# Every sixth partition: where the six blocks of two stacked operands lie in on-chip memory

## The reference, cut to what matters

```python
scores = jnp.einsum('bihd,bjhd->bhij', q, k) * d ** (-0.5)
scores = jnp.where(mask, scores, NEG)
p = jax.nn.softmax(scores, axis=-1)
o = jnp.einsum('bhij,bjhd->bihd', p, v)
```

## Time and profile before

| what | value |
|---|---|
| median of 3 runs | 423.71 us (423.14 to 424.17) |
| the profiled execution | 425.81 us |
| its span, from the first to the last instruction | 424.0 us |
| mean granted TensorE clock | 0.891 of full speed |
| busy in the span: TensorE, DVE, ACT, POOL | 314.1, 276.9, 164.7, 122.7 us |
| the queue of SP's DMAs | 42.12 MB in 50,211 packets |

### The profile page before, as it was taken

The page is one execution under the profiler, slowest core; times in us unless marked ns, Lnnn a source line. Parts: engine busy times, 40 slices in busy tenths (PEclk is TensorE's granted clock), DMA queues, the critical chain, the costliest instruction groups (busy, mean ns, idle before and its releaser), DMA issues. The chain is left out here.

```text
span 424.0 us, 5771 instructions
## 1 busy us (share of the span) xinstructions
PE 314.1 (74%) x1762; PEld 205.0 (48%) x1762; DVE 276.9 (65%) x865; ACT 164.7 (39%) x332; POOL 122.7 (29%) x105
## 2 busy tenths in 40 slices
PE   0797647628376479998899999997352988997982
PEld 0586546517143255555455555554341775444641
DVE  3868899565549188877614345354948959558694
ACT  1423512330012032322365665654302667757610
POOL 2654535547102011111104253343345000000023
PEclk9999879877568599999999999999795889898798
DMA  8992299968889837465543435006008000000011
GB/s 274 305 283 51 94 120 198 130 177 202 127 183 118 178 105 169 134 183 152 152 139 90 140 82 142 22 2 199 0 2 254 9 2 0 0 0 0 2 49 49
DMA packets 52545, 47.88 MB, mean 113 GB/s; under 512 B 5282, under 2 KB 50204, under 8 KB 52509
## 3 DMA queue, kind: packets, MB, share of 16 engines
q1 hardware_dynamic: 50211, 42.12, 43.4%
q0 software_dynamic: 1872, 4.22, 3.3%
q10 hardware_dynamic: 432, 1.18, 1.0%
HBM read 35.44 MB, written 15.87 MB: 121 GB/s over the span
## 5 line engine op out<-in xcount | busy, mean ns | idle before, releaser
L501 POOL DMA_INDIRECT yt_dram<-ysb,x x23 | 23.0, 1001 | 125.9 <-ACT ysb L617 87.2
L673 ACT ACTIVATE PT<-bank 128x512 f32<-128x512 f32 (+1 forms) x88 | 44.8, 558 | 21.5 <-PE bank L1177 20.8
L889 DVE TENSOR_REDUCE mx<-bank 128x1 f32<-128x384 f32 (+3 forms) x88 | 52.2, 637 | 1.2 <-PE bank L1159 0.5
L1158 PE MATMUL bank<-KS,QS 112*128 112x128 bf16 (+3 forms) x128 | 35.0, 322 | 12.9 <-DVE mx L889 11.6
L1032 DVE SCALAR_TENSOR_TENSOR s<-th,bank 128x176 f32<-128x176 f32 x23 | 7.7, 336 | 43.8 <-ACT th L705 43.7
L1788 PE MATMUL lbank<-u,w_ai 128*128 128x512 f32 x72 | 33.0, 619 | 1.9 <-issue 1.9
L1176 PE MATMUL bank<-QS,KS 115*128 115x512 bf16 (+3 forms) x128 | 31.1, 302 | 2.7 <-ACT PT L673 1.1
L1491 POOL TENSOR_TENSOR left<-xn,x 128x256 f32<-128x256 f32 x8 | 7.0, 898 | 86.7 <-DVE xn L1718 86.7
L507 POOL TENSOR_TENSOR small<-small,mhalf 128x16 f32<-128x16 f32 x8 | 24.4, 3046 | 17.3 <-DVE small L935 17.3
L1158 PEld LDWEIGHTS bank<-KS,QS 112*128 112x128 bf16 x128 | 12.7, 100 | 30.8 <-DVE mx L889 26.3
L1159 PE MATMUL bank<-tri,ident_b 128*128 128x128 bf16 x128 | 25.5, 227 | 0.0
(11 more groups left out here) (280 smaller groups left out, 808.7 us busy)
## 6 DMA issues: line engine op xcount, KB each, us to landing
wr<-w_dram SPq DMA_DIRECT2D x12, 352.0 KB
wt<-w_dram SPq DMA_DIRECT2D x11, 352.0 KB
QS<-parts_dram SPq DMA_DIRECT2D x12, 256.0 KB
KS<-parts_dram SPq DMA_DIRECT2D x12, 256.0 KB, 9.0
xs_dram<-x SPq DMA_DIRECT2D x1, 2967.0 KB, 15.3
x<-xs_dram SPq DMA_DIRECT2D x23, 129.0 KB, 2.2
w_dram<-in_w_chunks_dram SPq DMA_DIRECT2D x11, 256.0 KB, 4.8
wr<-in_w_chunks_dram SPq DMA_DIRECT2D x12, 176.0 KB
```

Source lines behind the costliest of these rows:

```text
L501: pool.indirect_dma_start(yt_dram, bass.IndirectOffsetOnAxis(ap=xg[:, n % XBUF, D:D + 1].bitcast(I32), axis=0), ysb[:, n % 2, :], None, bo ...
L673: act.activation(PT[:, k % 8, 0:n], bank[k % 2][:, 0:n], ACT.Exp, scale=float(DH) ** -0.5).then_inc(P_ready, 1)
L889: dve.tensor_reduce(mx[:, b * TB + i, heads[0]:heads[-1] + 1], bank[k % 2][:, 0:len(heads) * n].rearrange("p (h n) -> p h n", n=n), AX.X, ...
L1158: pe.matmul(out, QS[0:R_MAX, b, h, i * P:(i + 1) * P], KS[0:R_MAX, b, h, 0:n], start=True, stop=False)
```

## The change

The six blocks of 16 rows no longer take 16 neighbouring partitions each. Row d of block k goes to partition k + 6d in both stacks, so that the blocks interleave over partitions 0 to 95. Everything else, the rows from 96 on too, stays.

```diff
                     src = [parts_dram[b, which, level].rearrange("h d t -> d h t") for level in range(3)]
                     for block, (of_q, of_k) in enumerate(BLOCKS):
-                        rows = slice(block * DH, (block + 1) * DH)
+                        rows = slice(block, R_BIAS, len(BLOCKS))
                         if which == 0:
                             sp.dma_start(QS[rows, b, :, :], src[of_q]).then_inc(q_stacked[b], 16)
                         else:
                             sp.dma_start(KS[rows, b, :, :], src[of_k]).then_inc(k_stacked[b], 16)
```

## The result

The changed kernel takes 408.12 us (median of four executions, 407.47 to 409.56) against 423.42 for the kernel before on the same chip (421.56 to 424.17): a ratio of 0.965, 95% interval 0.961 to 0.969, so 15.3 us. The profiled execution takes 409.56 us with a span of 407.7, against 425.81 and 424.0: 16.3 us in the spans. The forecast was 405.0 in a range of 399.5 to 413.5. The sign, the places and the range hold; the size was 18.7 us against 15.3.

The account below looks back on a forecast made before the run. TensorE, idle three times behind slow stack DMAs to 16 neighbouring rows, was taken to bound the kernel. Gains of 5.2 + 5.9 + 7.6 = 18.7 us gave 407.1 profiled, 405.0 as median, range 399.5 to 413.5.

Parts of the forecast that it names:

- second place: TensorE's 6.81 us idle before 117.66, waiting for sorted rows behind the batch-1 queries; 5.9 us gain, 0.9 us left.
- One DMA: Each 256 KB stack DMA would take 0.95 us instead of 2.22, gaining 7.6 us per stack.
- the scaling by span: DMA time falls as its rows span more partitions: 0.68 us for 128, so 0.95 us for 91.
- rival A: Half the relief, as rows six apart still meet or SP's issue grows: 1.6 us a DMA, 413.3 us; chance 0.14.
- SP's issue: Issuing six stack DMAs, 2.78 to 3.01 us, assumed unchanged; it would decide only from 2.22 us per DMA.
- First place: TensorE's 8.31 us idle before 93.76, behind batch-0 stacks and delayed scatter sends; 5.2 us gain, 3.1 us left.
- SP's wait for the sends: SP's wait for the scatter's second half, before loading sorted rows, would end at 104.4 instead of 115.52.
- the wait at L1257: Sign: TensorE's wait at this line, for the sorted rows, would fall below 1 us.
- Third place: TensorE's 7.85 us idle before 143.79, for expert weights queued behind the batch-1 keys; 7.6 us further gain.
- The clock: TensorE runs at half clock after idling; shorter idle times might win 4 us in all, counted only in the lower bound.
- Rival B: Stride does nothing, the limit being each engine's long row run or reading 1 KB pieces; 423.7 us, chance 0.09.
- rival C: Slower: stepped rows dealt to eight engines instead of 16, 4.4 us a DMA; about 475 us, chance 0.05.

Follow-up runs that it names:

- The probe: Changed kernel plus nine appended series of DMAs on SP's queue, nothing beside them; span 500.0 us, six DMAs taking 15.6 us to neighbours, 9.8 six apart.

## Why the prediction was right, and where its size was off

The mechanism held at each of its places. The price of one DMA was off, and two steps of the second place; the total came out too large because the stacks gave less and the batch-1 keys started later than forecast.

- **One DMA.** Forecast 0.95 us, measured 1.34, and 5.2 us per stack in place of 7.6. The step that failed is the scaling by span, 0.68 x 128/91. The probe and the two-apart kernel show that span isn't the measure; the times go with how many rows fall on the same way in, two of the 16 for most steps, four for neighbours. The prediction had only two points, 16 neighbours and all 128 partitions, and drew a line between them; rival A named just this doubt, and the value lies between the forecast's 0.95 and A's 1.6, just beyond the forecast's 0.7 to 1.3.
- **SP's issue** was let stand, and grew from 0.45 to 0.61 us per DMA. As said, it decides nothing while the moving takes longer; but it takes 1.9 us more at the batch-1 queries.
- **First place:** forecast 5.2 us, measured 4.6. The sends were down by 81.1 (81.9 forecast), DVE's wait fell to 0.29 us, ACT's third cast of batch 1 starts 0.4 later (82.95).
- **Second place:** forecast 5.9 us more, measured 3.8, with 4.25 us left and not 0.9. Two steps failed, by 1.3 us each. SP reached the part writes 3.4 us earlier, as forecast (90.18), but from there to the stack's issue it took 8.0 us where it had taken 6.8, so the queries came at 98.23 and not at 96.9; why those 1.3 us were added stays open. And from their issue to the first transpose it took 11.0 us (17.3 before), not 9.7, because the stack's relief was smaller. The link by which the forecast went, SP's wait for the sends, was the wrong one: SP doesn't stand there any more (rows at 103.17, 104.4 forecast), and the rows wait for the stack in the transfers themselves, on either queue. Two of the prediction's signs failed: the wait at L1257 isn't below 1 us, and the wait after the batch-0 queries ended at 64.36, not about 62.
- **Third place:** forecast 7.6, measured 16.0 - 8.4 = 7.6, with 0.66 us left. That the two agree is luck. TensorE still stands 0.66 us here, so the product starts when the weights land, and they land 16.0 us sooner, not 18.7: the keys are issued 9.4 sooner (112.21; forecast 11.1), the stack takes 5.2 less (7.6), and the product follows the last landing after 5.2 in place of 6.6 us (no change forecast). This sum sets the whole lead; what the second place had failed to give came back here as a shorter wait, as the longer wait in the kernel with the rows on ACT shows the other way round.
- **After that** nothing was taken back: the lead of 16.0 at 127.78 is 16.3 in the spans, as a shift should be.
- **The clock** stood in the lower bound alone, and brought little. The four products behind the third idle time take 1.45 us where they took 2.71, but four products at 136.12, granted 0.50 (1.2 GHz) after TensorE's 2.09 us wait for DVE at 134.70, take 2.45 where those of their kind take 1.35 at the higher level. The mean granted clock went from 0.891 to 0.908.

One row was misread: slices 5 to 13 move 118 to 202 GB/s at a load of 60 to 90%; the 94 is slice 4, whose load is 20%. It changes nothing in the sum. Rival B falls with 204 GB/s in the stack's stretch; rival C with the time.

## What to carry to other kernels

Where a load fills a few partitions with long rows, look at the rate of its stretch against that of a load over all partitions, and try rows some partitions apart if the contraction allows any order. In these runs the time went with how many rows share a way into the SBUF, not with how far they spread. Then look at who is issued behind such a load: in this kernel the order in the queue was worth another 1 to 2% once the load itself was quick (0.965 to 0.945 with rows six apart, 0.963 to 0.948 seven apart; 408.12 to 403.85 us in the medians), and 1.4% while it was slow.

## What was not expected of the hardware

A DMA to stepped rows costs SP 0.61 us to issue, against 0.45 for neighbours of the same size. Rows issued on ACT's queue waited for a stack on SP's queue about as long as on the same queue (5.9 and 6.1 us, against 2.0 with no stack ahead). And eight neighbouring rows move at 61 GB/s, half of what 16 neighbours reach, though no other transfer runs.
